# A decoder layer in fp32: where the rotary products are formed, and how the attention weights are divided

## The reference, cut to what matters

```python
qkv = x @ qkv_w.T + qkv_b                     # 16 batches of 256 rows, 512 wide
q1, q2 = split(q); k1, k2 = split(k)          # halves of a head of 64
q = [q1 * cos - q2 * sin, q2 * cos + q1 * sin]   # the same for k
logits = (q . k) / 8, masked (causal, window 128)
e = exp(logits - max);  w = e / (sum(e) + exp(sink - max))
out = (w @ v) @ out_w.T + out_b
```

## Time and profile before

| | |
|---|---|
| median of 3 runs | 2067.29 us (2065.62 to 2067.77) |
| the profiled execution | 2068.88 us, of which the span of its instructions is 2067.1 us |
| granted TensorE clock, mean | 0.990 |
| busy share of the span | PE 95%, PEld 78%, DVE 78%, ACT 45%, POOL 38% |
| chain that ended last | PE 69%, DVE 20%, ACT 5%, issue 4%, POOL 1% |

### The profile page before, as it was taken

One profiled execution on the slowest core, in us unless ns is written; L12 is line 12 of the kernel. 1 busy time (PEld: TensorE's weight loads), 2 busy tenths in 40 slices (PEclk: granted clock), 3 DMA queues, 4 the chain that ended last, 5 costly groups with the idle time before them and its releaser, 6 DMA issues.

```text
span 2067.1 us, 45595 instructions
## 1 busy us (share of the span) xinstructions
PE 1963.5 (95%) x15488; PEld 1606.9 (78%) x15488; DVE 1609.0 (78%) x5780; ACT 928.8 (45%) x3481; POOL 781.9 (38%) x883
## 2 busy tenths in 40 slices
PE   5899999999999988989999999999998999999899
PEld 5688888888888867778888888888886677777687
DVE  4777877777778776667777777777777899999887
ACT  3555555555455544545555554554553222222233
POOL 3444434333333332322333323323322455555454
PEclk8999999999999999999999999999999999999999
DMA  5246211111111211111211111111104533232343
GB/s 174 75 103 144 73 52 63 52 52 70 55 52 62 85 61 58 48 50 64 80 54 52 53 52 52 53 63 52 52 33 170 164 101 89 86 87 87 98 143 123
DMA packets 71545, 162.25 MB, mean 78 GB/s; under 512 B 6657, under 2 KB 15233, under 8 KB 71185
## 3 DMA queue, kind: packets, MB, share of 16 engines
q1 hardware_dynamic: 62864, 142.54, 20.6%
q0 software_dynamic: 3840, 8.39, 2.2%
q10 hardware_dynamic: 4608, 8.39, 1.1%
HBM read 108.96 MB, written 50.41 MB: 77 GB/s over the span
## 4 chain that ended last, share of the span: by engine, by line
PE 69%; DVE 20%; ACT 5%; issue 4%; POOL 1%; DVEq 0%; DMA 0%; ACTq 0%; POOLq 0%
PE banks L504 17%; PE banks L564 14%; PE banks L519 9%; PE banks L1103 8%; PE banks L543 7%; PE banks L1309 4%; PE banks L497 4%; PE banks L529 4%; ACT pr L636 3%; DVE pr L849 3%; DVE m L825 2%; DVE terms L1135 2%; DVE banks L1149 2%; DVE pr L866 1%; DVE banks L1145 1%
## 5 line engine op out<-in xcount | busy, mean ns | idle before, releaser
L636 ACT ACTIVATE pr<-pr,mx 128x128 f32<-128x128 f32 x1024 | 399.0, 391 | 439.1 <-DVE mx L849 439.1
L710 POOL TENSOR_TENSOR m<-m,rope_sb 128x512 f32<-128x512 f32 x160 | 206.7, 1292 | 522.0 <-ACT m L623 522.0
L504 PE MATMUL banks<-xTh,wh 128*128 128x256 f32 x1280 | 378.9, 296 | 7.4 <-DVE xTl L809 4.0
L504 PE MATMUL banks<-xTl,wh 128*128 128x256 f32 x1280 | 365.4, 285 | 0.0
L504 PE MATMUL banks<-xTh,wl 128*128 128x256 f32 x1280 | 365.0, 285 | 0.0
L1103 PE MATMUL banks<-kv,tap 128*128 128x288 f32 x1280 | 323.9, 410 | 12.7 <-DVE res L1159 10.9
L1103 PEld LDWEIGHTS banks<-kv,tap 128*128 128x128 f32 x1280 | 238.1, 190 | 98.1 <-issue 36.5
L504 PEld LDWEIGHTS banks<-xTh,wh 128*128 128x128 f32 x1280 | 248.5, 194 | 11.3 <-issue 5.7
L504 PEld LDWEIGHTS banks<-xTl,wh 128*128 128x128 f32 x1280 | 249.0, 195 | 0.0
L858 DVE TENSOR_TENSOR den<-ac,es 128x4 f32<-128x4 f32 x256 | 52.2, 204 | 252.7 <-ACT es L639 252.7
L504 PEld LDWEIGHTS banks<-xTh,wl 128*128 128x128 f32 x1280 | 248.5, 194 | 0.0
(11 more groups left out here) (108 smaller groups left out, 3849.4 us busy)
## 6 DMA issues: line engine op xcount, KB each, us to landing
tap<-padded_taps SPq DMA_DIRECT2D x64, 256.0 KB, 3.3
kk<-in_ctxt SPq DMA_DIRECT2D x64, 192.0 KB, 3.4
x_in<-in_x SPq DMA_DIRECT2D x16, 512.0 KB, 4.0
xt_split<-xTh SPq DMA_DIRECT2D x16, 512.0 KB, 2.7
xt_split<-xTl SPq DMA_DIRECT2D x16, 512.0 KB, 3.8
xb<-in_x SPq DMA_DIRECT2D x16, 512.0 KB, 4.6
factors<-in_factors POOLq DMA_DIRECT2D x8, 1024.0 KB, 8.5
x_part_rows<-x SPq DMA_DIRECT2D x16, 512.0 KB, 3.0
```

The source lines that it names most:

```text
L504: last = pe.matmul(wP[:, h * T:(h + 1) * T], w[:, n, c, h * P:(h + 1) * P], a[:, s, c, :], start=(c == 0 and i == 0), stop=(c == KD - 1 an ...
L636: act.activation(pr[:, s, a, cols], pr[:, s, a, cols], ACT.Exp, bias=mx[:, s, i:i + 1], scale=-1.0, accum_out=ac[:, s, i:i + 1])
L710: pool.tensor_tensor(m2[:, s], m2[:, s], rope_sb[:, 1 if i == 0 else 0, 1:3], ALU.mult).then_inc(sin_ready, 1)
```

## The change

Three edits. In the first, `bent` goes from ScalarE and the product by sin goes from GpSimd. VectorE's `turned` now issues four scalar_tensor_tensor instructions instead of two, all out of `wP` with the bias and a table: two into `m1`, two into `m2` with the halves crossed. It waits for `qk_done` in place of `bent_ready`; GpSimd only adds. In the second, the division's four tensor_scalar instructions of 128x128 become one tensor_tensor of 128x512 with `rden` repeated along each quarter. In the third, `split_low` of the weights at the turn of the sweeps is called at the start of the following step, ahead of `residual`, and not at its own step's end.

```diff
-        def bent(y, p, i):
...
-            for half in range(2):
-                last = act.activation(m2[:, s, 1 - half], wP[:, half * T:(half + 1) * T], ACT.Identity,
-                                      bias=bqk_sb[:, y.sweep, i, half:half + 1])
-            last.then_inc(bent_ready, 1)
...
-            pool.tensor_tensor(m2[:, s], m2[:, s], rope_sb[:, 1 if i == 0 else 0, 1:3], ALU.mult).then_inc(sin_ready, 1)
-            pool.wait_ge(sin_ready, (QM + 1) * v + i + 1)
             pool.wait_ge(m_ready, (QM + 1) * v + i + 1)
...
-            wait_apart(dve, passed, (bent_ready, (QM + 1) * v + i + 1), (qr_ready, (QM + 1) * v + i - 1))
-            for half in range(2):
-                last = dve.scalar_tensor_tensor(m1[:, s, half], wP[:, half * T:(half + 1) * T], bias[:, half:half + 1],
-                                                tab[:, 0], ALU.add, ALU.mult)
+            wait_apart(dve, passed, (qk_done, (QM + 1) * v + i + 1), (qr_ready, (QM + 1) * v + i - 1))
+            for dst, h, half, f in [(m1, 0, 0, 0), (m1, 1, 1, 0), (m2, 0, 1, 1), (m2, 1, 0, 2)]:
+                last = dve.scalar_tensor_tensor(dst[:, s, h], wP[:, half * T:(half + 1) * T], bias[:, half:half + 1],
+                                                tab[:, f], ALU.add, ALU.mult)
             last.then_inc(m_ready, 1)
...
-            for a in range(2):
-                for t in range(NT):
-                    cols = slice(t * P, (t + 1) * P)
-                    i = 2 * a + t
-                    last = dve.tensor_scalar(pr[:, s, a, cols], pr[:, s, a, cols], rden[:, s, i:i + 1], None, ALU.mult)
-            last.then_inc(pn_ready, 1)
+            quarters = pr[:, s].rearrange("p a (t k) -> p (a t) k", t=NT)
+            dve.tensor_tensor(quarters, quarters, rden[:, s].unsqueeze(2).broadcast_to([P, 2 * NT, P]), ALU.mult).then_inc(pn_ready, 1)
...
+                    for i, n in split_last(y, p, j):
+                        split_low(i, n)
                     if residual_tile(y, p, j) is not None:
...
-                    for i, n in split_now(y, p, j):
-                        if not (y.first and n >= NU):
-                            split_low(i, n)
+                    if y.first:
+                        for i, n in split_now(y, p, j):
+                            if n < NU:
+                                split_low(i, n)
```

More of the change, by code:

```diff
@@ L111, in attention_part @@
 def attention_part(nc, ctx, space, conv, mix, x, wqkv, bqk, bv, wout, bout, sinks, rope, masks, ident, factors, ssm_pad,
-                   dcoef, x1_dram, q2_dram, pad_dram, x1_stored, x1t_stored, qk_done, v_done, m_ready, sin_ready, v_ready,
+                   dcoef, x1_dram, q2_dram, pad_dram, x1_stored, x1t_stored, qk_done, v_done, m_ready, v_ready,
                    qr_ready, masked, pt_masked, ot_lo, out_done, x1_ready, x1t_evac, f_in, tap_out):
@@ L199, in attention_part @@
     xt_loaded = [sem(f"xt_loaded{s}") for s in range(2)]
-    bent_ready = sem("bent_ready")
     s_done = sem("s_done")
@@ L310, in split_now, with split_last @@
         return []
+    def split_last(y, p, j):
+        k = 2 * p + j - 1
+        if y.first or y.number == 1 and k < 0:
+            return []
+        if k < 0:
+            return split_now(Body(y.m - 1, 0, y.number - 1), 7, 1)
+        return split_now(y, k // 2, k % 2)
     def placed(n, w, wo):
@@ L663, in scalar @@
         split_high(1, 1)
-        act.wait_ge(rope_in, 48)
         def body(y):
@@ L670, in body @@
                         p_evac(y, p, j)
-                    n = unit_of(p, j)
-                    if n is not None and n != V_UNIT and not y.drain:
-                        bent(y, p, rope_index(n))
                     if x_next(y, p, j):
@@ L706, in rotate @@
             s = (p // 4 + i) % 2
-            pool.wait_ge(bent_ready, (QM + 1) * v + i + 1)
-            if y.first and p == 0 and i == 0:
-                pool.wait_ge(rope_in, 48)
-            pool.tensor_tensor(m2[:, s], m2[:, s], rope_sb[:, 1 if i == 0 else 0, 1:3], ALU.mult).then_inc(sin_ready, 1)
-            pool.wait_ge(sin_ready, (QM + 1) * v + i + 1)
             pool.wait_ge(m_ready, (QM + 1) * v + i + 1)
@@ L973, in attention_part, with conv_part @@
     return Programs(sync, tensor, scalar, gpsimd, vector)
-def conv_part(nc, ctx, space, ctx_in, pad_dram, q2_dram, x1t_stored, qk_done, v_done, m_ready, sin_ready, v_ready, qr_ready,
+def conv_part(nc, ctx, space, ctx_in, pad_dram, q2_dram, x1t_stored, qk_done, v_done, m_ready, v_ready, qr_ready,
               masked, pt_masked, ot_lo, out_done, x1_ready, x1t_evac, tap_out, res_ready, res_placed):
@@ L1031, in first_loads @@
         sp.wait_ge(m_ready, NQK)
-        sp.wait_ge(sin_ready, NQK)
         sp.wait_ge(v_ready, NV)
@@ L1356, in decoder_layer @@
         m_ready = sem("m_ready")
-        sin_ready = sem("sin_ready")
         v_ready = sem("v_ready")
@@ L1369, in decoder_layer @@
         res_placed = sem("res_placed")
-        conv = conv_part(nc, ctx, space, ctxt, pad_dram, q2_dram, x1t_stored, qk_done, v_done, m_ready, sin_ready, v_ready,
+        conv = conv_part(nc, ctx, space, ctxt, pad_dram, q2_dram, x1t_stored, qk_done, v_done, m_ready, v_ready,
                          qr_ready, masked, pt_masked, ot_lo, out_done, x1_ready, x1t_evac, tap_out, res_ready, res_placed)
@@ L1374, in decoder_layer @@
                                    ssm_pad, dcoef, x1_dram, q2_dram, pad_dram, x1_stored, x1t_stored, qk_done, v_done, m_ready,
-                                   sin_ready, v_ready, qr_ready, masked, pt_masked, ot_lo, out_done, x1_ready, x1t_evac, f_in,
+                                   v_ready, qr_ready, masked, pt_masked, ot_lo, out_done, x1_ready, x1t_evac, f_in,
                                    tap_out)
```

## The result

The changed kernel takes 2109.97 us, the median of 4 runs (2109.19 to 2110.12), beside 2067.53 us for the kernel before on the same chip (2065.62 to 2068.94): a ratio of 1.0205, interval 1.019 to 1.022. It is slower by 42 us; the prediction was 2113. The profiled execution took 2109.89 us, with a span of 2108.1 and a mean granted clock of 0.990.

The account below looks back on a forecast made before the run. TensorE and the ring of VectorE and ScalarE, in balance, were taken to bound the kernel. The terms 25.7 + 6.5 - 4 + 17.5 = +45.7 us on the median of 2067.3 gave 2113 us, range 2090 to 2138.

Parts of the forecast that it names:

- The bound: VectorE's idle time is waiting inside a ring with ScalarE; rival that idle time absorbs the work: 2067 us, chance 5%.
- The gap between maxima and scores: TensorE's scores in steps 2 and 4 would wait about 1.5 and 0.6 us; staying at 0.2 would refute the ring.
- The price of the products: Rotation on VectorE: two more products cost +0.79 us in each of steps 0, 1, 3, 5 and 7.
- The price of the division: One product takes 0.60 us where four quarters took 0.79, saving 0.19 us in each of the 8 steps.
- The one product dearer than the four: Rival from the skill's cycle count: up to +2.2 us per window, up to 2170 us; anything above 2132 has 10%.
- the port: GpSimd's sums hold VectorE in step 2 of sweep 0, so no division saving there; at the turn 7.6 us go.
- Sweep 0: Eleven windows of +2.34 us each, 25.7 us, through lateness passed to TensorE's scores of steps 2 and 4.
- Sweep 1: Thirteen windows of +1.35 us each, 17.5 us, passed on to TensorE's scores of step 2.
- ScalarE's hop: Where turned waited for ScalarE's bent, 1.80 us becomes 1.58: -0.22 us in place of +0.79.
- Turn of the sweeps: Four windows, -4 us: rotations +15.8, divisions -6.1, the port -7.6, steps waiting for bent -5 and -1.
- Start and first three windows: First 53 us taken as 0; the three windows after it +2.15 us each, 6.5 us.
- Third edit: Low parts of weights: VectorE's stream is the same with and without it, so 0.

Follow-up runs that it names:

- the two places of the one instruction: Kernel before plus one unused VectorE instruction of about 0.6 us in each K or Q step: ahead of mask_min 2164.0 us, behind o_low 2073.2 us.
- rotation alone: Changed kernel with the division put back to four tensor_scalar instructions: 2138.94 us.
- Division alone: Kernel before with the division as one product, nothing else: 2059.1 us.
- ScalarE behind VectorE: Kernel before with one-product division, low parts a step later, bias sums waiting for step 2's division, and bent after turned in two Q units of sweep 1: 2023.13 us.
- moving the sums: Changed kernel with GpSimd's two bias sums of sweep 0 moved from step 2 to step 1, behind a wait for that step's division: 2099.26 us.
- a true step later: split_low called at the end of the following step: on the kernel before 2039.7 us, on the changed kernel 2089.4 us.
- the extra instruction ahead of the maxima: Kernel before with one unused bn_stats (0.60 us of VectorE) right ahead of mask_min in each step with a rotary unit: 2164.0 us.

## Why the prediction was right, step by step

**The bound.** Right. VectorE's idle time took up next to nothing of what was added ahead of the maxima: the two places of the one instruction show it, 96 us against 5. The gap between maxima and scores did not stay at 0.2 us; it is 0.6.

**The price of the products.** Right: 0.39 us each (1.56 for four). Where `turned` still waits, it is for TensorE's unit, as forecast (44.6 us in 47 waits, above).

**The price of the division.** Right: 0.60 to 0.61 us between starts. The one product dearer than the four, the rival, is refuted: with it, taking the one product out should have shortened the kernel, and rotation alone is 29 us longer. Of the two figures that the Trainium skill, "VectorE: DVE Perf Modes", section on the TRN2 errata, gave for that rival, the one product's 0.59 us agrees with the trace (0.60), and the four quarters' 0.51 does not (0.79). Without the double rate the same row would give 0.78, an estimate from its figures; no run here shows at which rate the quarters ran. The 256 products, grouped by line (shortest, median and longest ns):

```profile
L852 DVE TENSOR_TENSOR pr<-pr,rden x256: 691/692/696, 43.7 to 1616.7; 128x512 f32<-128x512 f32 x128
```

So an input repeated along the innermost 128 columns costs next to nothing, 0.692 us beside 0.681 for the same size out of PSUM, and as the longest took 0.696, no instance was held by the port.

**Sweep 0.** Forecast 49.19 us per window, measured 49.01. The step that failed in it is that GpSimd's sums would hold the division in step 2, near 1.5 us long: it took 0.69, and they held `xn` and `den`. That the size came out near is in part luck: either way VectorE is kept until GpSimd is through, and taking the hold away gave 0.67 us, but the forecast did not see that the sums would start earlier. The scores of step 2 wait 0.58 us, not 1.5: another part of the same lateness sits in the units ahead of them, which wait for `turned` (TensorE's weight loads for them, 4.2 us in 11 waits in this sweep). Which wait makes each of TensorE's other gaps, of 18.2 us idle in all, I did not separate.

**Sweep 1.** Forecast 48.87, measured 48.79. The sum was right, one reading in it was not: I took the 0.42 us for which the scores of step 4 wait as VectorE's, and also saw step 1 as without slack. Division alone, and ScalarE behind VectorE, showed ScalarE's hop behind the waits of steps 2 and 4 alike. In the change this hop disappears, in step 1 too, where I had counted nothing for it. A window came out 0.08 us shorter than forecast, as much as the wait that I read in step 1; that the one is the other was not tried.

**Turn of the sweeps.** Forecast -4, measured -1.1. The terms have the right signs: rotation alone makes the turn 5.0 us longer, and the division gives 6.1 back, as much as the -6.1 of the sum. What was mis-sized is the rotation's share with the port's and the hop's gains, +5.0 for the +2.2 worked out (15.8 - 7.6 - 6). The split is no finer than some microseconds, since TensorE's clock fell four times at the turn in the kernel before, three times in the changed one and for 17.1 us in all in rotation alone, and the forecast has no term for that.

**Start and first three windows.** Mis-sized: -2.5 us for 0 and +4.1 for +6.5. Rotation alone gives -1.8 at the start, so that the edit may gain something there; but kernels that leave the rotation as it was reach the first V between 51.7 and 53.3 us, so a good part of it can be chance, and which wait gains was not tried. In the three windows I had taken `den`'s hold by the port as unchanged; it was 2.33 us at 121.16 and is 1.81 there now, and moving the sums takes the three back to 143.7. How much of the rest of these stretches belongs to which wait I did not separate. The stages miss by +2.9 at the turn and by -7.6 in the others together, so that the total, +41.0 for +45.7, is a little nearer than its parts.

**Third edit.** Right: 0.

## What to carry to other kernels

Idle time of an engine that stands in a ring of waits is an answer it is waiting for, and is no room for more work: ask of each added instruction whether it stands ahead of or behind the one that others wait for. The same 150 instructions of 0.6 us cost 96 us ahead of the maxima and 5 us behind them.

A short wait in a bracket does not say that its cure is worth the bracket: look at what comes next behind it, here ScalarE's hop behind VectorE's. And of a move in the code, read the order of the instructions: the edit that was said to be a step later changed nothing, while a true step later gave 29 us.

## What the runs showed of the hardware

**TensorE's clock with the extra instruction ahead of the maxima.** Two windows of its sweep 1, from V's evacuation to the next, and two microseconds of a fall (columns as in the earlier trace rows; the granted clock is the figure before the last two):

```profile
1133.83:1183.77 49.94, 46.97 (x426) 39.13 (x426) 38.05 (x162) 23.94 (x100) 15.36 (x19) 1.00 0.15 54
1183.77:1235.26 51.49, 48.52 (x426) 39.99 (x426) 37.94 (x162) 23.95 (x100) 15.36 (x19) 0.97 0.15 52
1206.00:1208.00 2.00, 2.00 (x16) 0.77 (x8) 1.77 (x8) 0.38 (x3) 0.00 (x0) 0.50 0.03 8
```

The first window takes 49.9 us at full clock. In the second the clock falls to the 1.2 GHz level (0.50) for a stretch of 3.4 us, and it takes 1.55 us more, with the same work. There are ten such stretches in that sweep, and none in the changed kernel's, whose windows are a microsecond shorter and in which TensorE is busy for 96% of the sweep. Here it had been busy for some 94% of the time before the clock fell, with waits of up to 1.9 us for the maxima, where the changed kernel's longest is 1.6. The ten windows with a fall take 51.5 us each and the three without 49.9, so the clock costs some 16 us in this sweep. Why it fell in this kernel and not in the changed one was not tried.

**Four columns are held as long as 512.** `den`, two SBUF inputs of four columns, lasts 0.16 us alone, and 1.18 to 2.33 us beside GpSimd's sums (changed kernel, above, and the earlier trace rows); `xn`, with 512 columns, lasts 0.54 alone and 1.58 beside them.
